# A decoder kernel on one Trainium2 core: half of each q stack's transfers issued by ScalarE's queue

## The reference, cut to what matters

```
# 1  linear memory: state = 0.99 state + 0.01 v k^T; out_t = state q_t
x = layernorm(x + linear_memory(x) @ Wo.T + bo)
# 2  cross attention, 16 heads of 16
scores = einsum('bhqd,bhkd->bhqk', qh, kh) / sqrt(16); attn = softmax(scores)
x = layernorm(x + (attn @ vh) @ w_o.T + b_o)
# 3  self attention of the same shape, plus a mixture of 8 experts, 2 per token
gate = softmax(x @ W_gate + b_gate); combine = the two largest gates, others 0
x = layernorm(x + self_attention(x) + sum_e combine_e * (x @ W_experts[e] + b_e))
```

## Time and profile before

| | us |
|---|---|
| time, median of 3 runs (range) | 1286.24 (1284.12 to 1287.87) |
| the profiled execution's own time | 1286.56 |
| its span | 1284.8 |
| PE busy | 1219.4 (95%) |
| DVE busy | 904.3 (70%) |
| ACT busy | 775.6 (60%) |
| POOL busy | 371.6 (29%) |

### The profile page before, as it was taken

How to read it: one execution, slowest core, us unless ns; L and a number is a source line. 1 busy time by engine, 2 the same in 40 slices (tenths; PEclk the granted TensorE clock), 3 DMA queues, 4 the chain that set the end, 5 groups by cost and what they waited for, 6 DMA issues and landing times.

```text
span 1284.8 us, 19910 instructions
## 1 busy us (share of the span) xinstructions
PE 1219.4 (95%) x6912; PEld 599.4 (47%) x6912; DVE 904.3 (70%) x1823; ACT 775.6 (60%) x1077; POOL 371.6 (29%) x475
## 2 busy tenths in 40 slices
PE   8788989999999999999999999999999999998995
PEld 4333435454545445454454545444454534543542
DVE  2576886568777787767776787767877687667661
ACT  2255556666576665757557665666657576665674
POOL 6410004321621124320522206221153204331261
PEclk9999999999999999999999999999999999999997
DMA  8725034313333332234333143333223333303300
GB/s 258 125 43 92 18 51 68 50 22 73 58 67 51 50 77 43 50 50 68 67 67 58 20 75 67 67 52 46 53 44 44 51 51 51 67 2 51 50 19 17
DMA packets 50243, 74.92 MB, mean 58 GB/s; under 512 B 8536, under 2 KB 20320, under 8 KB 49888
## 3 DMA queue, kind: packets, MB, share of 16 engines
q1 hardware_dynamic: 48896, 72.72, 32.0%
q10 hardware_dynamic: 1248, 0.92, 0.4%
HBM read 18.04 MB, written 4.19 MB: 17 GB/s over the span
## 4 chain that ended last, share of the span: by engine, by line
PE 80%; DVE 7%; ACT 6%; issue 3%; POOL 1%; DMA 1%; ACTq 0%; SPq 0%; DVEq 0%; POOLq 0%
PE ms L423 37%; PE op L423 16%; PE sc L423 14%; PE mx L423 9%; DVE maxes L884 3%; ACT probs L722 2%; PE ms L473 2%; DVE k_parts L794 2%; ACT k_parts L661 1%; PE ms L528 1%; ACT moe L715 1%; DVE heads L857 1%; PE ms L523 1%; DMA w_ident<-in_ident 1%; DMA qs<-shift_r 0%
## 5 line engine op out<-in xcount | busy, mean ns | idle before, releaser
L884 DVE TENSOR_REDUCE maxes<-mx 128x1 f32<-128x512 f32 x1024 | 657.6, 684 | 209.2 <-PE mx L423 207.8
L722 ACT ACTIVATE probs<-sc 128x1024 f32<-128x1024 f32 x512 | 524.8, 1025 | 379.6 <-PE sc L423 373.2
L1062 POOL TENSOR_TENSOR x<-x,moe 128x256 f32<-128x256 f32 x256 | 187.7, 733 | 690.7 <-ACT moe L715 670.4
L423 PE MATMUL op<-probs,v 128*32 128x512 f32 x2048 | 275.4, 610 | 1.7 <-ACT probs L722 1.1
L423 PE MATMUL sc<-qs,ks 50*128 50x512 f32 x1024 | 257.1, 499 | 17.1 <-ACT probs L722 13.9
L423 PEld LDWEIGHTS sc<-qs,ks 50*128 50x128 f32 x1024 | 95.7, 183 | 315.7 <-ACT probs L722 238.8
L423 PE MATMUL mx<-ks,qs 48*128 48x512 f32 x1024 | 210.6, 407 | 19.4 <-DVE maxes L884 13.5
L715 ACT ACTIVATE moe<-ms,comb 128x256 f32<-128x256 f32 x256 | 107.1, 473 | 30.1 <-PE ms L423 30.1
L423 PEld LDWEIGHTS mx<-ks,qs 48*128 48x128 f32 x1024 | 97.7, 187 | 35.0 <-DVE maxes L884 25.7
L423 PE MATMUL ms<-we_hi,x2T_hi 128*128 128x512 f32 x256 | 93.7, 447 | 0.8 <-ACT o1T L660 0.4
L423 PEld LDWEIGHTS op<-probs,v 128*32 128x32 f32 x2048 | 40.5, 108 | 95.4 <-issue 94.0
(11 more groups left out here) (124 smaller groups left out, 1262.7 us busy)
## 6 DMA issues: line engine op xcount, KB each, us to landing
ks<-k_parts SPq DMA_DIRECT2D x192, 128.0 KB, 4.3
qs<-q_parts SPq DMA_DIRECT2D x189, 128.0 KB, 4.6
xT_s<-in_xT SPq DMA_DIRECT2D x8, 512.0 KB, 3.8
x_s<-in_x SPq DMA_DIRECT2D x8, 512.0 KB, 4.0
ctxT_s<-in_ctxT SPq DMA_DIRECT2D x8, 512.0 KB, 4.3
out<-x SPq DMA_DIRECT2D x7, 512.0 KB, 2.9
qs<-shift_r SPq DMA_DIRECT2D x128, 8.0 KB
probs<-in_we SPq DMA_DIRECT2D x1, 1024.0 KB, 7.1
```

The lines of the kernel that those rows point to most:

```text
L423: return nc.tensor.matmul(dst, lhsT, rhs, start=first, stop=last, skip_group_check=True)
L722: nc.scalar.activation(probs[:, (2 * s + h) % 3, :, :], sc[:], ACT.Exp).then_inc(exp_out, 1)
L884: nc.vector.tensor_reduce(maxes[:, g % 2, at:at + 1], mx[:, i % 3, :], AX_X, ALU.max).then_inc(max_out, 1)
L1062: nc.gpsimd.tensor_tensor(x2[:, n % 2, t, :], x2[:, n % 2, t, :], moe[:, k % 2, j * D:j * D + D], ALU.add).then_inc(acc, 1)
```

## The change

SyncE issues side 0 of a q stack only, in the half where it issued both. Side 1 goes to ScalarE's list, one half later, as `stack_q`, with the same waits and three issues. The first stack's ScalarE issue, written out before, moves into this list, and the copies of the expert weights in the prologue move with it by one half. The k stacks stay as they are.

```
@@ plan_others
                 for kind, name in zip("kq", names):
                     halves["sp"][at(f"{name}{c}", n) + 1].append(("stack_" + kind, 2 * PHASE[layer, n] + c))
+                    if kind == "q":
+                        halves["act"][at(f"{name}{c}", n) + 2].append(("stack_q", 2 * PHASE[layer, n] + c, None))
@@ sync, stack
-                for side in range(SIDES if (name, e) != ("q", 0) else 1):
+                for side in range(SIDES if name == "k" else 1):
@@ scalar, other
+                elif task == "stack_q":
+                    act.wait_ge(part_low["q"], k + 1)
+                    if k >= RING:
+                        act.wait_ge(score, 2 * 8 * (k - RING + 1))
+                        act.wait_ge(max_t, 32 * (k - RING + 1))
+                    for i in range(TERMS):
+                        act.dma_start(qs[64 + HD * i:64 + HD * i + HD, k % RING, :, :],
+                                      part["q"][64:128, Q_PART[i], :]).then_inc(stack_in["q"], 16)
@@ scalar, the loop over halves
-                if t == lin_at("qc0", 0) + 1:
-                    act.wait_ge(part_low["q"], 1)
-                    for i in range(TERMS):
-                        act.dma_start(qs[64 + HD * i:64 + HD * i + HD, 0, :, :],
-                                      part["q"][64:128, Q_PART[i], :]).then_inc(stack_in["q"], 16)
+                if t == lin_at("qc0", 0) + 2:
                     act.wait_ge(we_in, 16 * DC)
```

## The result

| | before | after |
|---|---|---|
| time, median of 4 runs (range), us | 1285.20 (1284.12 to 1287.87) | 1304.26 (1302.66 to 1315.32) |
| ratio, with its 95% interval | | 1.0163 [1.0133, 1.0193] |
| profiled execution: time, span | 1286.56, 1284.8 | 1304.98, 1303.2 |

The change makes the kernel 19.1 us slower (1.6%). The prediction had said 1297.1 us, an addition of 10.9 us. The direction and the mechanism were right; the size was a good 8 us too small, so that the result lies at the upper edge of the forecast's own range (1290 to 1304).

A forecast was written before the change was run, and what follows sets the result against it. TensorE, busy 95%, was taken as bound together with ScalarE through a shared score buffer. Pushes at the q stacks summed to 10.9 us on 1286.2, giving 1297.1 us (+0.8%); own range 1290 to 1304, 8-in-10 range 1287 to 1314.

The forecast's parts named there:

- The start of the group: ScalarE's three issues start when q's low part is ready or the copy ahead is released, beside the running activation.
- `moe` stack: One of six q stacks where a `moe` copy stands ahead of ScalarE's issues; forecast +0.69 us each.
- `lin` and `x2T_hi` stacks: Five q stacks each with a `lin` or `x2T_hi` copy ahead of ScalarE's issues; forecast +0.07 and +0.19 us each.
- Rival 1: ScalarE's issue starts only when its activations have drained; 27 us added, 1313 us; chance 0.17.
- The price of a group: Three issues cost ScalarE's instruction stream 2.17 us, measured once in the prologue; 67 us over 31 stacks.
- Rival 2: Not slower: idle time hides issues costing 1.6 us or less a group; 1286 us, between 1284 and 1288; chance 0.20.
- What the group delays: Behind the issues wait `oT` with TensorE's values product, and the next exponential, priced 0.50 us after `oT`.
- nothing ahead: Five q stacks with no copy ahead of ScalarE's issues; forecast +0.30 us each.
- The stack at 1044.71: The last batch's stack, where ScalarE has no idle time before the exponential; forecast +1.54 us.
- The irregular stacks: Four stacks in the short tables of the first and last batch; forecast some +0.6 us each, 2.4 in all.
- `shift_r` and the start: TensorE's 2.4 us of waits for `shift_r`, the larger ending at 121.73; forecast from 0 to -2.4 us, taken as 0.
- Rival 3: Both queues take turns at the descriptor generator; a group takes about 3.7 us, 42 us on top, 1339 us; chance 0.06.

The follow-up runs named there:

- one_issue: Against the changed kernel, ScalarE issues one of the three side-1 transfers of each q stack after the first, SyncE the other five; 1285.34 us, ratio 1.0001.
- two_issues: Against the changed kernel, ScalarE issues two of the three side-1 transfers of each q stack after the first, SyncE the other four; 1291.33 us, ratio 1.0039.
- behind_oT: Against the changed kernel, ScalarE's three issues stand behind the copy oT of the same half, not ahead of it; 1290.37 us, ratio 1.0045.
- spread: Against the changed kernel, ScalarE's three issues stand in three different halves, one to a half (first stack all at once); 1288.94 us, ratio 1.0030.
- back_1044: Against the changed kernel, the one stack near 1044 us (stack 27) is issued whole by SyncE again; 1301.15 us, ratio 1.0110.
- sp_late: Against the changed kernel, SyncE instead of ScalarE issues side 1, at the same later half slot (first stack as before); 1284.75 us, ratio 0.9990.
- two_back: Against the changed kernel, stacks 3 (near 117 us) and 26 (at 1003 us, by mistake for 27) are issued whole by SyncE; 1306.61 us, ratio 1.0161.
- even_half: Against the changed kernel, ScalarE's group of three issues stands one half later, in an even half (odd for two irregular stacks); 1289.99 us, ratio 1.0034.
- six_issues: Against the changed kernel, ScalarE issues all six transfers of each q stack behind the first, SyncE none; 1397.82 us, ratio 1.0849.

## Why the prediction was right, and where it was too small

**The start of the group** (an issue runs beside the activation ahead of it): right. Two small delays were missing: at the `moe` stack the issue starts 0.10 us after the copy, where I had let both start together, and at the `lin` and `x2T_hi` stacks 0.13 after SyncE's issue. Rival 1 (after the activations have drained) is false.

**The price of a group**, 2.17 us: right, and the term that I was least sure of. From the first issue to `oT` it is 2.17 at the `moe` stack (482.02 to 484.19), 2.10 at the `lin` and 2.11 at the `x2T_hi` one, 2.58 at the long one. Of the 96 issues the shortest takes 0.55 us, the median 0.62, the longest 1.24. Rival 2 needed 1.6 us for three.

**What the group delays**: this term of the sum was sized too small. I priced the next exponential, 0.50 us behind `oT`. The values product waits for `oT` itself and begins 0.74 us behind `oT`'s start; before, it began 0.12 us behind the exponential, which by my sum would have been 0.62. The shortfall of each kind comes out of these small terms: `moe` 0.69 + 0.10 + 0.12 = 0.91; `lin` 0.07 + 0.13 - 0.07 + 0.12 = 0.25; `x2T_hi` 0.19 + 0.13 - 0.06 + 0.12 = 0.38; nothing ahead 0.30 + 0.05 + 0.12 = 0.47 (0.05 for the 2.22 us from issue to `oT` that such a group takes when it is not the long one). Each is within 0.02 us of the ledger. About 0.2 us a place is little, but the pushes are small remainders after idle time: with the 0.36 more of the long group, these 21 stacks cost 11.3 us where I had 6.9. That is over half of the shortfall.

**The stack at 1044.71**: the wait was right (forecast 1.54; `op` comes 1.58 us later behind SyncE's issue), but not what follows. The timeline of the kernel after there:

```profile
1057.08 1.83 SPq L373 DMA_DIRECT2D qs<-q_parts  x3
...
1059.32 0.60 ACT L662 ACTIVATE oT<-op 128x512 f32<-128x512 f32 x1 [1.49 <-issue]
...
1060.06 1.06 PE L425 MATMUL op<-probs,v 128*32 128x512 f32 x8 [1.85 <-ACT oT L662]
1061.05 0.23 PEld L425 LDWEIGHTS sc<-qs,ks 50*128 50x128 f32 x2 [0.84 <-ACT probs L724]
1061.05 0.74 PE L425 MATMUL sc<-qs,ks 50*128 50x512 f32 x2
```

`op` there in the kernel before:

```profile
1046.11 1.06 PE L423 MATMUL op<-probs,v 128*32 128x512 f32 x8 [0.27 <-ACT oT L660]
```

The pair of score products takes 0.74 us instead of 0.50. The windows behind the place, first of the kernel after, then of the kernel before at the same work:

```profile
1061.00:1065.00 4.00, 4.00 (x48) 2.41 (x48) 1.64 (x4) 1.51 (x3) 0.00 (x0) 0.57 0.75 87
```

```profile
1047.00:1051.00 4.00, 4.00 (x56) 1.86 (x52) 3.50 (x8) 2.34 (x4) 0.00 (x0) 1.00 1.10 134
```

The granted clock is 0.57, close to the lower level (1.2 of 2.4 GHz), after a wait of 1.85 us. That is the other 1.5 us. I priced a wait at its own length.

**The irregular stacks**: 2.2 where I had said 2.4 (0.8, 0.6, 0.6 and 0.2). The sum is near, but I had some 0.6 for each, so part of that is luck.

**`shift_r` and the start**: forecast 0, measured 1.8 us in the first 245 (without the 0.2 of the stack near 205). Of this, 0.4 is the wait near 120 us: 2.06 us in the kernel after, 1.67 before. It is 1.99 to 2.07 in one_issue, two_issues, behind_oT, spread and back_1044 too, and 1.68 in sp_late. But it does not follow ScalarE's transfers: it is 1.83 in two_back, where SyncE issues this stack alone, 1.84 in even_half, where ScalarE issues nothing between 115 and 132 us, when TensorE's wait is over, and 1.62 in six_issues, where ScalarE issues all six. What makes it longer stays open.

The other 1.4 us fit the clock. In the first 245 us TensorE runs 13.7 us at half clock before and 17.1 us after, and not at the same places: before it has two such stretches (near 77 and 217 us) that the kernel after has not, after it has one near 123 and two that are longer (near 44 and 187). Behind the wait near 120 the clock (121.40 to 125.00) is 1.00 before and 0.65 after. But it is 0.67 in sp_late, which waits 1.68 us, and 1.00 in behind_oT, which waits 2.07. At this place a dip comes and goes with no tie to the length of the wait or to ScalarE's issues that these runs show; what decides it stays open. By the prediction's own sign (a change of TensorE's time outside the 31 places) this was a part that the forecast did not have; its size may be the chance of one execution. The same kernel shows such a spread: the changed kernel's four runs take 1300.9, 1301.7, 1303.2 and 1313.5 us of span at mean clocks of 0.987, 0.988, 0.984 and 0.974.

**Rival 3** (two queues take turns at the descriptor generator): false. SyncE's three issues take 1.82 and ScalarE's 2.06 us side by side, and ScalarE's six alone 3.81. Only a rare long group could be such a meeting (2.75 beside 2.48 at 521.26; in two_back 2.58 beside 2.85 near 672), and at the first of these SyncE's six were long before the change too, 4.51. What makes a group long is not shown.

**SyncE's freed 1.9 us, 31 times**: worth nothing, as counted: no place in the ledger gains by it, and in sp_late, where SyncE issues the same three half a slot later, no steady place loses. (TensorE's other waits for landings, which the prediction passed over, are for weights in the first 12 us, 2.2 us at most, and the change leaves them alone.)

## What to carry to other kernels

A DMA issue moved to a compute engine costs that engine's instruction stream 0.6 to 0.7 us each (3.81 us for six, 2.06 for three), and the cost begins where the group is longer than the idle time at that very half slot: read the slack there, not the engine's mean load (60% here). Look at everything that stands behind the issue in program order, and price the first dependent of each; here `oT`, not the exponential, was late first. If ScalarE must issue, one transfer for a stack was free in this kernel (one_issue), three in three half slots cost 3.8 us (spread), and a group costs least behind the copy that another engine waits for, 5.2 us (behind_oT), or one half later, 4.8 us (even_half); no version was measurably faster than leaving all six on SyncE, whose queue had the time.

## What the runs showed of the hardware beside this

- A DMA issue on ScalarE's queue runs beside the activation ahead of it (from 0.10 us after its start at the `moe` stack, from 0.03 us before it at the `x2T_hi` one) but holds all that comes behind it, with 0.1 us from the end of the last issue to the next activation.
- The duration of an issue mostly does not depend on the other queue: 1.82 to 1.83 us for SyncE's three with ScalarE's three beside them, 3.75 for six alone; a rare group is long in both (2.75 and 2.48 at 521.26).
- TensorE's granted clock can fall to the lower level behind a wait, and the length of the wait alone does not decide it. Such a stretch followed waits of 1.85 us (at 1057), of 1.21 (two_issues, the same place) and all of 2.58 and more in six_issues, but only eight of its fourteen of about 2.0 to 2.1. Of the waits of about 0.84 us at the `moe` stacks one was followed by it, in two_back (the wait ends at 942.22; the clock from 944 to 948 is 0.60). Near 120 us the same wait of about 2 us was followed by a dip in some executions and not in others.
